# Graph attention and a mixture of experts on one core: row sums of four layers by products with a ones stationary, biases folded into the features

## The reference

```
feat      = x W                                (256 x 256)
e[h,n,m]  = leaky_relu(self[h,n] + neigh[h,m], 0.2) - 1e10 (1 - adj[n,m])
alpha     = softmax over m of e
out       = elu(alpha @ feat + b)              (b: one value per head and feature)
```

## Time and profile before

| | us |
|---|---|
| median of 3 runs | 403.03 (402.68 to 407.12) |
| the profiled execution | 402.71 |
| its span, first to last instruction | 401.0 |
| busy: PE, DVE, ACT, POOL | 375.3, 253.4, 218.2, 81.9 |

### The profile page before, as it was taken

How to read it: one execution, slowest core, us unless ns; L and a number is a source line. 1 busy time by engine, 2 the same in 40 slices (tenths; PEclk the granted TensorE clock), 3 DMA queues, 4 the chain that set the end, 5 groups by cost and what they waited for, 6 DMA issues and landing times.

```text
span 401.0 us, 8488 instructions
## 1 busy us (share of the span) xinstructions
PE 375.3 (94%) x2840; PEld 333.2 (83%) x2841; DVE 253.4 (63%) x834; ACT 218.2 (54%) x516; POOL 81.9 (20%) x92
## 2 busy tenths in 40 slices
PE   8797898896998999999999999999999999999991
PEld 7576777685887888888888889999999999999981
DVE  3999989999977988882764514444444444444430
ACT  3989999887578647421111146555554545454310
POOL 5246320001000000007152001131313131313131
PEclk9789999998999999999999999999999999999996
DMA  6449297604023000199797220323232333332121
GB/s 183 196 168 447 77 334 316 262 16 203 2 90 124 2 0 28 18 399 418 284 384 255 37 45 27 41 40 41 43 41 40 40 41 41 43 41 29 23 21 20
DMA packets 30501, 48.72 MB, mean 122 GB/s; under 512 B 18640, under 2 KB 27008, under 8 KB 27520
## 3 DMA queue, kind: packets, MB, share of 16 engines
q1 hardware_dynamic: 25152, 41.92, 30.1%
q0 software_dynamic: 4080, 5.18, 8.3%
q10 hardware_dynamic: 1232, 1.15, 0.9%
HBM read 39.46 MB, written 8.77 MB: 120 GB/s over the span
## 4 chain that ended last, share of the span: by engine, by line
PE 76%; DVE 13%; ACT 7%; issue 2%; POOL 0%; POOLq 0%; DVEq 0%
PE ps_c L816 20%; PE ps_o L834 12%; PE ps_c L673 12%; PE ps_pt L680 6%; PE ps_n L816 5%; DVE weights L1115 5%; PE ps_pt L590 4%; PE ps_n L673 4%; DVE weights L1132 3%; ACT weights L916 3%; PE ps_o L605 3%; PE ps_n L680 2%; PE ps_c L566 2%; ACT weights L922 1%; PE ps_f L579 1%
## 5 line engine op out<-in xcount | busy, mean ns | idle before, releaser
L816 PE MATMUL ps_c<-tile_t,weights 128*128 128x128 f32 x736 | 89.5, 275 | 0.0
L816 PEld LDWEIGHTS ps_c<-tile_t,weights 128*128 128x128 f32 x736 | 87.6, 192 | 1.2
L1182 DVE SCALAR_TENSOR_TENSOR gate_silu<-gate_tanh,ps_c 128x256 f32<-128x256 f32 x76 | 31.8, 419 | 82.0 <-ACT gate_tanh L1021 66.9
L497 POOL DMA_INDIRECT out<-y_sb,tile_in x23 | 35.7, 1554 | 146.6 <-DVE y_sb L1376 146.6
L916 ACT ACTIVATE weights<-weights 128x256 f32<-128x256 f32 x128 | 63.2, 498 | 0.8 <-DVE weights L1132 0.7
L673 PE MATMUL ps_c<-x_norm_t,weights 128*128 128x256 f32 x240 | 56.6, 383 | 1.3 <-DVE hidden L1185 1.3
L1026 ACT ACTIVATE weights<-weights 128x2560 f32 x23 | 53.7, 2337 | 7.1 <-issue 7.1
L1115 DVE SCALAR_TENSOR_TENSOR weights<-weights 128x256 f32<-128x256 f32 x128 | 54.5, 487 | 1.7 <-ACT weights L903 1.5
L834 PE MATMUL ps_o<-weights,hidden 128*128 x230 | 53.6, 380 | 0.6 <-DVE hidden L1185 0.6
L1021 ACT ACTIVATE gate_tanh<-ps_c 128x256 f32<-128x256 f32 x46 | 17.6, 384 | 63.1 <-PE ps_c L816 63.1
L673 PEld LDWEIGHTS ps_c<-x_norm_t,weights 128*128 128x128 f32 x240 | 44.2, 190 | 7.8 <-DVE hidden L1185 1.5
(11 more groups left out here) (188 smaller groups left out, 486.7 us busy)
## 6 DMA issues: line engine op xcount, KB each, us to landing
weights<-w_routed SPq DMA_DIRECT2D x8, 1920.0 KB, 14.2
weights<-t_rows SPq DMA_DIRECT2D x14, 1024.0 KB, 6.4
weights<-w_shared SPq DMA_DIRECT2D x1, 3840.0 KB, 16.7
tile_in<-slots SPq DMA_DIRECT2D x92, 32.0 KB, 1.8
slots<-pad_row SPq DMA_DIRECT2D x1, 1188.0 KB, 11.4
slots<-pad_row SPq DMA_DIRECT2D x8, 132.0 KB, 3.5
weights<-x SPq DMA_DIRECT2D x2, 256.0 KB, 3.5
x_in<-x SPq DMA_DIRECT2D x2, 256.0 KB, 4.2
```

What stands on the lines that cost most here:

```text
L497: pool.indirect_dma_start(out=out, out_offset=bass.IndirectOffsetOnAxis(ap=tile_in[:, slot, ID_COL:ID_COL + 1].bitcast(U32), axis=0), in_= ...
L816: mm = pe.matmul(ps_chunk[c][:, part * cw + i * P:part * cw + (i + 1) * P], ring[r % RING][:, a:a + P], tile_t[:, r % 2, k, :], start=(k = ...
```

## The change

- Row sums of layers L = 0 to 3 (`SUMS_BY_PRODUCT = 4`): after its eight products, `weigh` makes eight more with a stationary of ones (128x32, `ones_cols`) on the same moving operand into `ps_sum` (the second bank of `ps_c`), so that the sums stand in the layout of `ps_o`, repeated over the 32 features. `divide` of these layers takes the reciprocal of 512 columns of `ps_sum` into `invb`. `invert_sums`, `spread_inverse` and `copy_inverse` of these layers are gone, and so are the accumulations of their exponents. Layers 4 to 7 keep the old way.
- Biases: alpha sums to 1 in each row, so the bias may be added to the features. For first layers it is a 65th row of `w0_sb` against a row of ones in `ctx_sb`; for second layers GpSimd adds a bias tile to `feat` (`add_bias`, two operations of 128x256 for each of L = 3, 5, 6, 7), and `weigh` waits for it (`feat_biased`).
- The elu: ScalarE does one exponential of 512 columns and then a relu of 1 - exp of 512; VectorE's `end_elu` is max(v, -that) and `divide` no longer has the two operations with bias columns. VectorE's two small operations that prepared bias columns at w = 0 are gone.
- `IDLE_FIRST` is 3 for 8. One small load of the bias row stands in SP's queue ahead of the gates', and the bias tile's load replaces that of the bias columns.

```diff
 QUADS = HEADS // QUAD
+SUMS_BY_PRODUCT = 4
 PAIR_HEADS = 2
 WIDE_BANKS = HEADS // PAIR_HEADS
-IDLE_FIRST, IDLE_EACH = 8, 4
+IDLE_FIRST, IDLE_EACH = 3, 4
...
 AHEAD = 4
+def spread_to(L):
+    return max(0, L + 1 - SUMS_BY_PRODUCT)
+def second_layers_to(L):
+    return sum(1 for at in range(L + 1) if second_layer(at))
...
         ps_chunk = (ps_c[:, 0, :], ps_c[:, 1, :], ps_n)
+        ps_sum = ps_c[:, 1, :]
         ps_wide = (ps_c.rearrange("p a n -> p (a n)"), ps_pt)
...
             sp.dma_start(w0_sb[0:F_IN, :], w0).then_inc(ld_w0, 16)
+            sp.dma_start(w0_sb[F_IN:F_IN + 1, :], bias_rows[0:1, :]).then_inc(ld_w0, 16)
             sp.dma_start(gates_sb, gates.rearrange("(o d) -> o d", o=1).to_broadcast([P, 2])).then_inc(ld_gates, 16)
...
             sp.dma_start(w1_sb, w1.rearrange("(k p) n -> p k n", p=P)).then_inc(ld_w1, 16)
-            sp.dma_start(bias[:, 0, :], bias_t).then_inc(ld_bias, 16)
+            sp.dma_start(bias_wide, bias_rows[1:2, :].to_broadcast([P, D])).then_inc(ld_bias, 16)
             sp.dma_start(router_w, w_router.rearrange("(k p) e -> p k e", p=P)).then_inc(ld_router, 16)
...
                 make_mask(n, n % PAIR)
-            for n in range(B):
+            def add_bias(L):
+                pool.wait_ge(feat_copied, L + 1)
+                for m in range(HV):
+                    v = feat[L % PAIR][:, m, :]
+                    pool.tensor_tensor(v, v, bias_wide, ALU.add).then_inc(feat_biased, 1)
+            pool.wait_ge(ld_bias, 16)
+            add_bias(layer_of(0, 1))
+            power(B, 0)
+            copy_rows(0)
+            add_bias(layer_of(1, 1))
+            add_bias(layer_of(2, 1))
+            power(B + 1, 1)
+            copy_rows(1)
+            add_bias(layer_of(3, 1))
+            for n in range(PAIR, B):
                 power(B + n, n % PAIR)
...
                 if L >= PAIR:
-                    pe.wait_ge(invb_copied, L - 1)
+                    pe.wait_ge(invb_copied, spread_to(L - PAIR))
                 src = feature_sources(L)
+                if ORDER[L][1] == 0:
+                    pe.wait_ge(ones_ready, PAIR + 1)
+                    src = [(ctx_sb[ORDER[L][0] % PAIR][0:F_IN + 1, :], w0_sb[0:F_IN + 1, :], None)]
                 for half in range(HV):
...
                     pe.wait_ge(feat_copied, L + 1)
+                    if second_layer(L):
+                        pe.wait_ge(feat_biased, HV * second_layers_to(L))
                     if L > 0:
...
                                        start=(m == 0), stop=(m == HV - 1))
+                if L < SUMS_BY_PRODUCT:
+                    for m in range(HV):
+                        for i in range(QUAD):
+                            mm = pe.matmul(ps_sum[i * FO:(i + 1) * FO, quad * N + half * P:quad * N + (half + 1) * P], ones_cols,
+                                           probs_t[:, w % 2, (i * HV + m) * P:(i * HV + m + 1) * P],
+                                           start=(m == 0), stop=(m == HV - 1))
                 if u == UNITS - 1:
...
-                pe.wait_ge(sums_inverted, L + 1)
+                pe.wait_ge(sums_inverted, spread_to(L))
                 pe.wait_ge(feat_copied, min(L + 2, STREAM))
-                if L > 0:
-                    pe.wait_ge(invb_copied, L)
+                pe.wait_ge(invb_copied, spread_to(L - 1))
                 for quad in range(QUADS):
...
                     ins = act.activation(v, v, ACT.Exp, bias=neg_max[:, w % AHEAD, i:i + 1], scale=-1.0,
-                                         accum_out=sums[:, L % PAIR, s:s + 1])
+                                         **({} if L < SUMS_BY_PRODUCT else {"accum_out": sums[:, L % PAIR, s:s + 1]}))
                 ins.then_inc(probs_ready, 1)
...
             def copy_inverse(L):
-                act.wait_ge(invb_turned, L + 1)
+                act.wait_ge(invb_turned, spread_to(L))
                 if L > 0:
...
                 act.wait_ge(o_read, L + 1)
-                for quad in range(QUADS):
-                    ins = act.activation(att_exp[:, quad, :], att[:, quad, :], ACT.Exp, bias=bias_col(0, ORDER[L][1], quad))
-                ins.then_inc(exp_ready, 1)
+                act.activation(att_exp, att, ACT.Exp).then_inc(att_exped, 1)
+                act.wait_ge(att_exped, L + 1)
+                act.activation(att_exp, att_exp, ACT.Relu, bias=1.0, scale=-1.0).then_inc(exp_ready, 1)
...
-                c = L % PAIR
                 dve.wait_ge(o_ready, L + 1)
-                dve.wait_ge(invb_copied, L + 1)
+                if L < SUMS_BY_PRODUCT:
+                    link(dve.reciprocal(invb.rearrange("p a n -> p (a n)"), ps_sum))
+                else:
+                    dve.wait_ge(invb_copied, spread_to(L))
                 dve.tensor_tensor(att, ps_o.rearrange("p (a n) -> p a n", a=QUADS), invb, ALU.mult).then_inc(o_read, 1)
-                dve.wait_ge(o_read, L + 1)
-                for quad in range(QUADS):
-                    ins = dve.tensor_scalar(elu[c][:, quad, :], att[:, quad, :], bias_col(1, ORDER[L][1], quad),
-                                            bias_col(2, ORDER[L][1], quad), ALU.max, ALU.add)
-                link(ins)
...
                 n, layer = ORDER[L]
-                c = L % PAIR
                 dve.wait_ge(exp_ready, L + 1)
-                dst, done = (h0_t[n], h0_ready) if layer == 0 else (elu[c], h1_ready)
-                dve.scalar_tensor_tensor(out=dst, in0=att_exp, scalar=1.0, in1=elu[c], op0=ALU.min, op1=ALU.add).then_inc(done, 1)
+                dst, done = (h0_t[n], h0_ready) if layer == 0 else (elu[L % PAIR], h1_ready)
+                dve.scalar_tensor_tensor(out=dst, in0=att_exp, scalar=-1.0, in1=att, op0=ALU.mult, op1=ALU.max).then_inc(done, 1)
...
             dve.memset(x_norm_t[0], 0.0).then_inc(zeros_ready, 1)
+            dve.memset(ones_cols, 1.0).then_inc(ones_ready, 1)
+            for c in range(PAIR):
+                dve.memset(ctx_sb[c][F_IN:F_IN + 1, :], 1.0).then_inc(ones_ready, 1)
             weigh_columns(0)
...
                 slots_now = filler_slots(w)
-                if u == 3:
+                if u == 3 and L >= SUMS_BY_PRODUCT:
                     invert_sums(L)
...
                     weigh_columns(1)
-                if w == 0:
-                    dve.wait_ge(ld_bias, 16)
-                    dve.tensor_scalar(bias[:, 1, :], bias[:, 0, :], -1.0, None, ALU.mult)
-                    link(dve.tensor_scalar(bias[:, 2, :], bias[:, 0, :], -1.0, None, ALU.add))
                 if w == UNITS:
```

More of the change, by code:

```diff
@@ L141, in gate_col, with build @@
     return 2 * c0 + i * P - c0, 2 * c0 + cw + i * P - c0
-def build(nc, x, ctx_t, w0, w1, first_cols, w1_t, gates, bias_t, w_router, w_routed, w_shared, t_rows, slots, out):
+def build(nc, x, ctx_t, w0, w1, first_cols, w1_t, gates, bias_rows, w_router, w_routed, w_shared, t_rows, slots, out):
     with ExitStack() as stack:
@@ L218, in build @@
         invb = carve([P, QUADS, N], until="tail")
-        bias = carve([P, 3, LAYERS * QUADS], until="tail")
+        bias_wide = carve([P, D], until="tail")
         stats = [carve([P, HV, 8], until="tail") for c in range(PAIR)]
@@ L226, in build @@
         rows = [[carve([P, HV, ROW], until="tail") for k in range(TOPK)] for n in range(PAIR)] + late_rows
-        def bias_col(kind, layer, quad):
-            a = layer * QUADS + quad
-            return bias[:, kind, a:a + 1]
         ps_c = bank("ps_c", [P, 2, 512])
@@ L269, in build @@
         h0_ready, h1_ready, h1_turned, h1_read = sem("h0_ready"), sem("h1_ready"), sem("h1_turned"), sem("h1_read")
-        ld_bias, bias_ready = sem("ld_bias"), sem("bias_ready")
+        ld_bias, ones_ready, feat_biased = sem("ld_bias"), sem("ones_ready"), sem("feat_biased")
+        att_exped = sem("att_exped")
         x_norm_ready, x_norm_turned, x_norm_copied = sem("x_norm_ready"), sem("x_norm_turned"), sem("x_norm_copied")
@@ L313, in build @@
         pad_row = sb("pad_row", [P, ROW])
+        ones_cols = sb("ones_cols", [P, FO])
         zero_row = sb("zero_row", [P, D])
@@ L729, in _ @@
             nodes(1)
-            pe.wait_ge(ld_w0, 16)
+            pe.wait_ge(ld_w0, 16 * 2)
             features(0)
@@ L776, in _ @@
             shared_piece(1, FILLED)
-            pe.wait_ge(invb_copied, STREAM)
+            pe.wait_ge(invb_copied, spread_to(LAST))
             ranks(0, ps_f)
@@ L967, in _ @@
                 slots_now = filler_slots(w)
-                if u == 0 and L > 0:
+                if u == 0 and L > SUMS_BY_PRODUCT:
                     copy_inverse(L - 1)
@@ L1458 @@
         "gates": np.concatenate([np.asarray(g_xattn).reshape(-1), np.asarray(g_ffn).reshape(-1)]),
-        "bias_t": np.stack([np.asarray(L0_xattn_b0), np.asarray(L0_xattn_b1)]).reshape(LAYERS * QUADS, P).transpose(1, 0),
+        "bias_rows": np.stack([np.asarray(L0_xattn_b0).reshape(D), np.asarray(L0_xattn_b1).reshape(D)]),
         "w_router": np.asarray(L0_ffn_w_router).transpose(1, 0),
```

## The result

| kernel | median (runs) | ratio to before, 95% interval |
|---|---|---|
| before | 403.95 us (5; 402.68 to 407.58) | |
| changed | 414.84 us (5; 413.93 to 422.42) | 1.0266 [1.0212, 1.0320] |
| changed, seven more runs | 415.72 us | 1.0272 [1.0223, 1.0321] |

Slower, by 10.9 us; 7.2 were forecast. Medians here are of all executions of a kernel; the ratios leave out executions more than 1.5% above its fastest. The profiled execution took 417.83 us (span 416.0, clock 0.969), 3 us above the median. TensorE's stretch at half clock is in it, so places up to the seam are compared in it, and what lies behind the seam in other runs.

The account below looks back on a forecast made before the run. VectorE, with ScalarE close behind, was taken to bound the kernel until about 97 us, then TensorE. 402.7 + 7.9 at the seam - 0.5 behind it = 410.1, 410.4 against the median; stated 410.2, range 406.3 to 414.5.

Parts of the forecast that it names:

- the seam: Where TensorE idles 3.25 us at 96.80 until VectorE has spread layer 4's inverse; forecast: TensorE leaves it at +7.9.
- The start term: At the kernel's start, five fewer zero products let VectorE begin earlier: -1.6 us, taken between bounds of 1.0 and 2.0 to 2.4.
- rival 4: At the start, the shorter start does nothing or harms: +1.6 us, 411.8; chance 0.1.
- Reciprocal: VectorE's division in layers 0 to 3: a reciprocal of 512 columns takes 3.53 us, at 6.6 ns a column.
- Rivals 1 and 3: VectorE's wide reciprocal: first, dearer than the slope, 4.4 us, 413.6, chance 0.17; second, cheap, so not slower, chance 0.14.
- The loop over `o_read`: From one division to the next, `weigh` waits for the reciprocal; TensorE's loop 16.7 us, under VectorE's 17.4 by 0.7.
- Rival 2: At `weigh` of w = 4L + 4, that loop becomes the bound: one us for each of layers 1 to 3, 413; chance 0.15.
- Layer 1's division to the seam: VectorE's stretch through layers 2 and 3: +2.67 at layer 1, +4.1 for layers 2 and 3, +0.5 for GpSimd's `add_bias`.
- Behind the seam: Layers 4 to 7, TensorE-bound: part of its 1.28 us wait at 130.08 for VectorE comes back, -0.5, bounds 0 and 1.3.

Follow-up runs that it names:

- the faster kernel: Biases in the features and new elu, no sums by product, eight first zero products, nine more before layer 4's transposes, against the kernel before: 400.15 us, 0.9918.

## Why the prediction was off, point by point

The direction was right, and so were the cost of the wide reciprocal and the place where it is handed on. The step that failed is the start: a gain was forecast, and a loss came. The clock behind TensorE's waits stood in no term. The terms in turn:

- **The start term failed.** Forecast: "between them -1.6", and the first division at 33.1. Measured: 36.18. The weights' products came early, but the products behind them ran at half rate. ScalarE's copies of the first wide products began at 6.88 us for 7.41, the second pair of them already at 9.44 for 8.72, and the store of layer 1's rows to memory (SyncE, `t_rows`) issued at 17.0 instead of 12.9. VectorE then waited 1.40 us for these rows; in the run with eight first products and the clock kept up, the store issues at 13.3 and the wait is gone. With eight first products the first reciprocal starts at 34.93: so three cost 1.25 us at that place in these two profiles, where 1.6 less was forecast, together 2.9. On the kernel before the short start costs 2.2 us by itself. It was rival 4, at 1.6 above the forecast and a chance of 0.1. It had the right rows, 236 ns for a zero product at the start and 145 later, and gave them too little weight: 1.6 us and one case in ten, where 2.9 came. In four of the seven profiles with three first products the half rate lasts longer still, and layer 0's division comes near 41.
- **Reciprocal**: 3.53 forecast, 3.36 measured, 0.17 less in each of four. The slope of the widest rows (6.6 ns a column) held to 512 columns: 6.37. Rivals 1 and 3 fall with it. The estimate of 8.3 ns from the Trainium skill ("VectorE: DVE Perf Modes", Walkthrough, eight repeats, with the page's clock) is not borne out by the trace: 6.37.
- **The loop over `o_read`** from layer 0 to 1: 14.3 forecast (37.4 to 51.7), 14.27 measured (40.27 to 54.54). The waits of 2.60 here and 2.46 at a clock of 1.00 were in the forecast, and at that clock ScalarE sets the pace, as it said. Rival 2 did not come in the forecast's form: no wait before layers 2 and 3. But its condition, a TensorE loop over 13.1 us, was met at layer 1 in the two executions where the clock stayed at 0.50 for some 10 us: about 17.4 us, and waits of 6.07 and 6.02.
- **Layer 1's division to the seam**: 104.7 - 51.7 less the same stretch before, +7.2 forecast, +7.47 measured. In it is GpSimd's `add_bias`, beside which VectorE's masked maxima take twice their time (GpSimd's and VectorE's timelines):

```profile
64.20 1.49 POOL L498 TENSOR_TENSOR weights<-weights 128x256 f32<-128x256 f32 x2 [8.60 <-ACT weights L907]
...
64.34 0.85 DVE L1167 CUSTOM_DVE_ANT_0 weights<-weights 128x256 f32<-128x256 f32 x1
...
65.13 0.85 DVE L1167 CUSTOM_DVE_ANT_0 weights<-weights 128x256 f32<-128x256 f32 x1
...
65.91 0.41 DVE L1167 CUSTOM_DVE_ANT_0 weights<-weights 128x256 f32<-128x256 f32 x1
```

  0.86 for this pair and as much for the second, at 105.33 us right before the seam: +1.7 against +0.5 for both. Three reciprocals took 0.5 less than forecast, so the agreement of 7.47 with 7.2 is in part luck. Leaving the additions out of the faster kernel moved its time by nothing that could be told.
- **Behind the seam**: -0.5 forecast. TensorE's wait of 1.28 is 0.38 now, so 0.9 comes back. What was missing is the clock, put at nothing: a wait of 4.63 us is followed by 12 us at 0.50, and the profiled execution loses 3.8 us between the seam (+11.1) and the first routed product (239.0 to 253.9, +14.9). In the median it is less: keeping TensorE busy gives 2 to 4 us, and 1.5 on the kernel before, which has a low stretch there of its own.

Together: the forecast's 104.7 at the seam plus 2.9 at the start and 0.3 after it is 107.9, the measured place. In the time, the change was +10.9 for +7.2, and these 3.2 are most of the 3.7 that were missing. The 410.2 with 3.2 more is 413.4; of the last 1.4, 0.9 is that the kernel before measured 403.95 here and 403.03 when the forecast was made. What is left, 0.5, is less than the runs spread, and that it is the clock's part is not shown: the median execution has no profile.

## What to carry over

An operation whose price grows with its width should run on the narrow sums before they are spread: here 16 columns cost 0.25 us and the copy 0.43, and 512 cost 3.36 on the engine that sets the pace. A wait of TensorE has a second price, the slow stretch behind it, so look at the granted clock behind each long wait before crediting a gain, and try products that nobody reads in it. Take more than one profile where executions spread: the same kernel had its first division at 36.18 and at 40.92. Zero products at a start are not idle work to be trimmed: look at how long the first real products take.

## What the runs showed of the hardware

- The granted clock can read 1.00 while products take twice their time: 2.07 against 1.13 us for the same four at the start. It was so in all seven profiles with three first products, and in three of nine with eight. It ended at about 21.7 us in one profile of the changed kernel and at about 32 in another. The Trainium skill ("TensorE: Matmul & The Clock Gate", Seeing it yourself) warns that the clock's records have been unreliable; this case's rows agree.
- After waits of 2.95 us and 4.63 us, each behind a stretch in which TensorE was partly idle, it ran at 1.2 GHz for some 10 and 12 us. The length of the wait alone does not give that of the stretch: 3.25 us in the kernel before was followed by some 3.5 us at 1.2 GHz, and 2.29 at layer 0's division in the changed kernel by some 3. With zero products in the waits it stayed at 2.4.
- A reciprocal costs VectorE 6.37 ns a column from 256 to 512, nearly five times a multiplication of the same 512 (3355 and 688 ns).
- While GpSimd adds 128x256 tiles, a masked maximum of 128x256 on VectorE takes 0.85 us for 0.42.
